# A fifth late batch in a gated cross-attention and mixture-of-experts kernel, with one product of the batches between moved by a pass

## The reference

```python
ifg = concat([q, k, v]);  ig = ifg @ igate_w.T + igate_b;  fg = ifg @ fgate_w.T + fgate_b
cs = cumsum(log_sigmoid(fg));  log_D = tril(cs[s] - cs[t]) + ig[t]
C = (q_h @ k_h.T / sqrt(64)) * exp(log_D - max(log_D))          # 8 heads of width 64
h = (C / (max(|sum C|, exp(-max)) + 1e-6)) @ v_h;  attn = layernorm(h) * ln_scale
x = x + tanh(g_xattn) * attn                    # q = layernorm(x), k = v = ctx
y = layernorm(x)
routed = sum over the 2 best experts of gate * (silu(y @ w_gate) * (y @ w_up)) @ w_down
shared = (silu(y @ shared_gate) * (y @ shared_up)) @ shared_down      # width 512
out = x + tanh(g_ffn) * (routed + shared)
```

## Time and profile before

| | us |
|---|---|
| median of three runs | 1143.31 (1141.41 to 1145.24) |
| profiled execution | 1135.05 |
| its span, first to last instruction | 1133.2 |
| TensorE busy | 1025.1 (90%) |
| VectorE busy | 761.3 (67%) |
| GpSimd busy | 419.3 (37%) |
| ScalarE busy | 386.4 (34%) |
| mean granted clock of TensorE | 0.949 |

### The profile page before, as it was taken

One profiled execution on the slowest core, in us unless ns is written; L12 is line 12 of the kernel. 1 busy time (PEld: TensorE's weight loads), 2 busy tenths in 40 slices (PEclk: granted clock), 3 DMA queues, 4 the chain that ended last, 5 costly groups with the idle time before them and its releaser, 6 DMA issues.

```text
span 1133.2 us, 20738 instructions
## 1 busy us (share of the span) xinstructions
PE 1025.1 (90%) x6395; PEld 859.9 (76%) x6395; DVE 761.3 (67%) x1983; ACT 386.4 (34%) x854; POOL 419.3 (37%) x309
## 2 busy tenths in 40 slices
PE   4689999999999988989895599999999999999882
PEld 2578988898889877868684478888888888887661
DVE  2888889888888887878766544444444444444766
ACT  2644444444443444435421123233323333231010
POOL 4010221222112221222215536558656676204675
PEclk9889999999999998989976899999999999999986
DMA  7340210222012202120107744564555554836888
GB/s 259 149 164 1 76 71 9 82 75 76 20 56 76 75 38 80 52 94 38 75 38 260 265 135 167 176 207 158 170 195 193 168 176 149 325 112 186 285 288 272
DMA packets 60036, 155.60 MB, mean 137 GB/s; under 512 B 7296, under 2 KB 7296, under 8 KB 58016
## 3 DMA queue, kind: packets, MB, share of 16 engines
q0 software_dynamic: 18448, 69.22, 17.6%
q1 hardware_dynamic: 29008, 62.93, 16.1%
q10 hardware_dynamic: 12480, 22.16, 5.5%
HBM read 93.46 MB, written 60.82 MB: 136 GB/s over the span
## 4 chain that ended last, share of the span: by engine, by line
PE 80%; DVE 5%; issue 4%; DMA 4%; POOL 3%; ACT 2%; SPq 1%; ACTq 0%; POOLq 0%; DVEq 0%; another core or an unknown queue 0%
PE bank L1260 19%; PE bank L1125 12%; PE bank L1278 10%; PE bank L1030 5%; PE bank L1136 5%; PE bank L1053 4%; PE bank L993 4%; PE bank L1248 3%; POOL w_ring L694 3%; PE bank L1074 3%; PE bank L1077 3%; PE bank L1075 3%; PE bank L1322 2%; PE bank L1062 2%; PE bank L1269 2%
## 5 line engine op out<-in xcount | busy, mean ns | idle before, releaser
L1260 PE MATMUL bank<-w_ring,x2nT 128*128 x948 | 241.8, 404 | 1.7 <-DVE x2nT L1829 1.7
L1260 PEld LDWEIGHTS bank<-w_ring,x2nT 128*128 128x128 f32 x948 | 174.3, 191 | 37.7 <-issue 2.4
L1125 PE MATMUL bank<-x2nT,w_ring 128*128 128x256 f32 x1152 | 148.5, 285 | 0.0
L563 POOL DMA_INDIRECT routed_x<-x2n,slot_u x64 | 65.8, 1029 | 222.8 <-DVE slot_u L1593 207.0
L1125 PEld LDWEIGHTS bank<-x2nT,w_ring 128*128 128x128 f32 x1152 | 141.0, 191 | 0.3
L1811 DVE SCALAR_TENSOR_TENSOR ctxT<-ctxT,bank 128x256 f32<-128x256 f32 x79 | 33.3, 421 | 138.7 <-ACT ctxT L921 138.7
L1278 PE MATMUL bank<-w_ring,sh_actT 128*128 x474 | 123.7, 396 | 1.1 <-DVE sh_actT L1824 1.1
L648 POOL TENSOR_TENSOR w_ring<-area,one 128x3072 fp32r<-128x3072 f32 x14 | 74.2, 5303 | 115.5 <-PE bank L1278 115.5
L1278 PEld LDWEIGHTS bank<-w_ring,sh_actT 128*128 128x128 f32 x474 | 88.9, 188 | 22.5 <-issue 1.4
L651 POOL TENSOR_TENSOR w_ring<-area,w_ring 128x3072 fp32r<-128x3072 f32 x14 | 95.6, 6832 | 2.5 <-POOL w_ring L648 2.5
L921 ACT ACTIVATE ctxT<-bank 128x256 f32<-128x256 f32 x79 | 30.3, 384 | 189.9 <-PE bank L1260 189.9
(11 more groups left out here) (224 smaller groups left out, 2052.8 us busy)
## 6 DMA issues: line engine op xcount, KB each, us to landing
routed_y<-cs_in ACTq DMA_DIRECT2D x79, 256.0 KB, 2.3
x2n<-routed_x SPq DMA_DIRECT2D x75, 256.0 KB, 2.9
base_out<-in_x_dram SPq DMA_DIRECT2D x16, 512.0 KB, 5.0
cs_in<-in_ctx_dram SPq DMA_DIRECT2D x16, 512.0 KB, 4.0
area<-n_L_ffn_expert_gate_dram POOLq DMA_DIRECT2D x16, 512.0 KB, 4.7
area<-in_L_ffn_expert_up_dram POOLq DMA_DIRECT2D x16, 512.0 KB, 6.3
area<-n_L_ffn_expert_down_dram POOLq DMA_DIRECT2D x16, 512.0 KB, 7.7
out_dram<-base_out SPq DMA_DIRECT2D x32, 256.0 KB
```

Of the source, the lines that this page charges most:

```text
L563: pool.indirect_dma_start(out=routed_x, in_=x2n[:, b.par, j, :], in_offset=None, out_offset=bass.IndirectOffsetOnAxis(ap=slot_u[:, b.par, ...
L1125: last = mm(gu_bank(b.n, m)[:, at:at + S], w[:, w_part, c, m * P:(m + 1) * P], x2nT[:, x_part, c, :], start=(c + p == 0), stop=(c == DC - ...
L1260: last = mm(bank[2 + t.par][:, :], xtT[:, x_part, t.par, c * P:(c + 1) * P], w_gu[:, bass.ds(slot, 1), w_part, c, :].rearrange("p a i -> p ...
```

## The change

Batch 7 becomes a fifth late batch, so that EARLY is 0 to 6, 8, 10, 12 and 14. For the early batches that are followed by a late one (`CARRY`: 6, 8, 10 and 12; not 14, the last) down product 1 is no longer made in the pass in which the batch is H, but in the next one, behind the spreads of heads 0 and 1, at the place where piece 2 stands in other passes; VectorE adds it there too. In the late stage there are ten tiles instead of eight; the kept activations of the last three late batches are loaded ahead of gathers 8, 15 and 22, and VectorE's list of output tiles is a new one. The stores of `kept_x` become five, by the same code.

```diff
-LATE = (9, 11, 13, 15)
+LATE = (7, 9, 11, 13, 15)
...
+CARRY = tuple(b for b in EARLY if b + 1 in LATE and b != LAST)
...
-LATE_LOADS = [9, 16]
+LATE_LOADS = [8, 15, 22]
...
 # tensor and vector, step():
                 if rest:
                     shared(H, 2)
+                if t.n - 3 in CARRY:
+                    shared_down(H + -1, 1)
...
-                if rest:
+                if rest and H.n not in CARRY:
                     shared_down(H, 1)
...
 # vector, late stage:
-            for u, (some, more) in enumerate(((1, 2), (2, 2), (1, 2), (2, 2), (2, 2), (1, 2), (2, 2)), 1):
+            for u, (some, more) in enumerate(((1, 2), (1, 2), (1, 2), (1, 2), (1, 2), (1, 2), (2, 2), (1, 2), (1, 2)), 1):
                 late_gate(u)
                 late_rest(u - 1)
                 late_up(u)
```

## The result

The changed kernel took 1151.95 us (median of 4), the kernel before 1142.36 beside it: ratio 1.0079, interval 1.0042 to 1.0115. It is slower by 0.8%. The time lies 0.05 us inside the range; the likeliest case, the forecast's 1140 to 1150 us, did not come, and the third rival did, with a larger price. The profiled execution took 1148.17 us (span 1146.6), 13.1 more than that of before.

What follows compares the result with a forecast made beforehand. TensorE was taken to bound the kernel up to 403 us, no engine alone the late stage. Terms -5.5 + 0 + 7.1 = +1.6 us gave 1136.7 for a profiled execution, 1144.9 beside the median; range 1130 to 1152.

Steps and rivals of the forecast that it cites:

- the forecast: Whole kernel: +1.6 us, 1144.9 us beside the median; chance 0.42 for 1140 to 1150 us.
- rival 3: Late stage: the added load comes too late behind gather 21; +6.5 us in all, 1149.8 us; chance 0.24.
- signs of being wrong: Granted clock of 1.00 in the stretches beginning with one down product, or late-stage loads that end no wait.
- Batch 7 leaves: Attention part: two stretches of 37.0 us become one of each alternating kind, 34.26 and 34.21; -5.5 us.
- Extra store and ScalarE's wait: Attention part: storing batch 7's x2nT, and ScalarE's wait for it a pass later, cost 0.
- Carried product: Passes with the later second down product: idle time and clock fall only move; 0, ends 4.0 less or 4.7 more per stretch.
- Rival 1: Attention part: the clock holds, three stretches of -4.0 and -2 for the last pass; 1130.9 us; chance 0.22.
- Two more tiles: Late stage: ten tiles with load waits end +7.1 us later; ends -11.5 and +12.
- the loads: Late stage: loads behind gathers 7, 14, 21 land at 1059.1, 1080.6, 1105.1; the last two waits 3.9 and 5.4 us.
- the upper end: Late stage: 8.64 us for both loads, +2.1 after each, 1 to 2 us more VectorE waiting for gathers; +12.
- Rival 2: Late stage: loads land in 4.0 us each, so the stage is -3.9; 1133.9 us in all; chance 0.12.

Runs made afterwards that it cites:

- carry4: The kernel before (four late batches) with only the second down product of batches 8, 10 and 12 made one pass later; ratio 0.9988 to the kernel before.
- act4: The kernel before (four late batches) with its two later loads issued by ScalarE instead of GpSimd; ratio 0.9976 to the kernel before.
- nocarry5: The changed kernel with the second down product of batches 6, 8, 10, 12 made in its own pass again; ratio 1.0045 to the kernel before.
- pooladded: The changed kernel with only the added load moved, ahead of gather 17 instead of 22; ratio 0.9987 to the kernel before.
- best5: The changed kernel with ScalarE's later loads, the carried product cut in two, and VectorE's pairs two ahead of the sum, one behind; ratio 0.9870 to the kernel before.
- noload5: The changed kernel without its three later loads, so batches 11, 13, 15 use the activations of 7 and 9; ratio 0.9940 to the kernel before.
- act5split: The changed kernel with the later loads issued by ScalarE and the carried product cut in two; ratio 0.9900 to the kernel before.

## Why the prediction was right, and where it failed

The time lies inside the range, by 0.05 us, and that is luck: the forecast was +1.6 us, the medians beside each other are 9.6 apart, and the range reached so far only for rival 3. Neither of its signs of being wrong came: the clock in the stretches concerned is 0.90, and the loads end three waits. The sum failed in one term, the two more tiles.

- *Batch 7 leaves, -5.5*: right. From 329 us on two stretches of 37.0 became 33.8 and 34.2, -5.9, of which the carried product's 0.4 is a part. Two later ones are 0.5 and 0.6 shorter and the last pass 0.6 longer, so the marks give -6.2 up to the last router product. ("Up to 403 us every stretch takes 37.0 us" holds from the fourth gate product on; the first three take 25.8, 26.7 and 34.2.)
- *Extra store and ScalarE's wait, 0*: nothing in the traces speaks against it.
- *Carried product, 0*: right as far as the ratios tell (carry4, 0.9988), and by its mechanism. The wait is 2.47 (forecast 2.5), the fall moved into it; it lasts 6.8 us, not 10, and the stretch is 0.5 shorter than that of before. Rival 1 (the clock holds) is out.
- *Between the parts*: no step spoke of it, and it is +2.4. All ten traces with a carried product have 421.4 to 422.6 us there, three of the four without it 419.1 to 419.6, act4 422.3. Some 1.3 us of it lie ahead of the end of the first experts' wait for their rows, 5.88 us (4.14 before), and 1.1 behind. The wait alone isn't it: carry4 has 3.53 and 421.5 in all. The cause stays open.

```profile
649.47 1.12 PE L1252 MATMUL bank<-ident,x2n 128*128 128x128 f32 x4 [5.88 <-DMA x2n<-routed_x]
```

- *Two more tiles, +7.1, at most +12*: this term failed; it was +17.2. In nocarry5 and carry4, with the late stages of after and before, the difference is 11.4, so the size is uncertain by some us, but both are above the forecast. The step that failed is the loads: waits of 0.4, 3.9 and 5.4 us were forecast, and 3.34, 4.80 and 7.17 came. From the stage's start the loads were to be issued after 25.3, 46.0 and 70.5 us, and were after 27.0, 50.7 and 78.7. The loop hands each slip on to the next load: tiles 4, 6, 8 start 3.2, 5.7 and 9.0 us later than forecast, the end is 10.1 later. Of these, 3.0 are landings (8.33, 8.58, 8.41 where 6.86 and 7.75 were taken) and 3.3 half clock behind the waits (none was taken for the first, where it cost 1.5; 2.7 each for the others instead of 1.5 and 2.1). Another 1.8 are gathers issued later ahead of the first load, and 1.4 belong to the third load. There the forecast let gather 21 wait for pair 17 alone, but GpSimd was held up at gather 19 and had six issues ahead of the load. The last 0.6 lie at the end. The landing of 6.86 and the mean of two were the wrong choice, and the upper end raised only the last two loads, not the first.
- Rival 2 (loads land sooner) is out: 8.3 to 8.6 us for the three later loads, where it had 4.0. The Trainium skill's fit ("DMA: Bandwidth & Descriptors", section "Anatomy of one DMA — SWDGE (gpsimd) path") gives an estimate of 4.4 us for them. Of the five loads of 1 MB none was that quick:

```profile
DMA to landing us min/median/max: 5.4/8.3/8.6
```

- Rival 3 named the mechanism rightly: the added load comes too late, behind gather 21. It got the second-largest chance and too small a price, and the two other loads were late as well.

Sum: -6.2 + 2.4 + 17.2 = +13.4 us of span, against +1.6. What stays open: the second stretch of 2.4, the carried product's few us up to the late stage, the stalls of 5 to 9 us in the late stage, and the clock with the cut product in an execution that starts at full clock.

## What to carry to other kernels

Where a load stands in an in-order queue behind work that waits for the load's own consumer, an error of a microsecond is handed on to every later load (here 3.2, 5.7 and 9.0 us); count the turns, and put the load where its buffer comes free. When a batch of work is added at the end of a tuned pipeline, list which positions in other engines' orders were chosen for the old pace. Here moving three numbers turned +0.8% into -0.8%.

## What had not been expected of the hardware

- The same placement gives a clock fall of different length from pass to pass: uncarried stretches of 30.8, 31.6 and 34.3 us in one execution (nocarry5).
- In pooladded and best5 VectorE and ScalarE go on 5 and 8 us after the products they wait for, within 0.06 us of each other; in noload5 and act5split ScalarE does so alone, 8 to 9 us after. The traces name no releaser.
- Where the traces have its landing, a load of 1 MB from `kept_x` took 5.1 to 6.0 us ahead of the gathers and, but for one of 6.86, 8.0 to 8.9 among them.
